# Two layers of graph attention on 4096 nodes: node rows grouped by partition, and the scale of the exponentials computed on another engine

## What is computed

```
h = relu(layernorm(x))                                   # per row of 128
cos = beta * (h @ h.T) / (norm(h) @ norm(h).T + 1e-7)
P = softmax(cos + (1 - adj) * -1e9, axis=1)              # only edges count
x = x + P @ h
h = relu(layernorm(x))
x = x + h @ W_self + (adj @ h / max(rowsum(adj), 1)) @ W_neigh
```

## Time and profile before

| | |
|---|---|
| Time, median of 3 runs | 494.0 us (493.81 to 495.3) |
| Profiled execution | 493.64 us, span 491.8 us |
| TensorE busy | 467.5 us, 95% of the span |
| VectorE, ScalarE, GpSimd busy | 281.5, 285.3, 288.5 us |
| Granted TensorE clock | 0.999 of full speed |
| Moved by DMA | 74.37 MB in 31548 packets |

### The profile page before, as it was taken

The page is one execution under the profiler, slowest core; times in us unless marked ns, Lnnn a source line. Parts: engine busy times, 40 slices in busy tenths (PEclk is TensorE's granted clock), DMA queues, the critical chain, the costliest instruction groups (busy, mean ns, idle before and its releaser), DMA issues.

```text
span 491.8 us, 12379 instructions
## 1 busy us (share of the span) xinstructions
PE 467.5 (95%) x5200; PEld 391.3 (80%) x5200; DVE 281.5 (57%) x675; ACT 285.3 (58%) x425; POOL 288.5 (59%) x250
## 2 busy tenths in 40 slices
PE   1869999999999999999999999998999999999997
PEld 1737888888787887888878877886787888888886
DVE  6977756657566585566855675775766410122222
ACT  2998778775886767966589669777864100000000
POOL 3899988876986768975699569767762000000000
PEclk9999999999999999999999999999999999999999
DMA  8246964456676445855567556655300000000000
GB/s 251 105 130 221 313 253 178 174 213 197 216 291 217 176 139 196 290 199 189 176 227 256 158 194 216 212 195 175 107 5 0 13 13 23 23 23 23 23 23 21
DMA packets 31548, 74.37 MB, mean 151 GB/s; under 512 B 2560, under 2 KB 15104, under 8 KB 31488
## 3 DMA queue, kind: packets, MB, share of 16 engines
q1 hardware_dynamic: 31488, 73.54, 43.8%
HBM read 71.43 MB, written 2.10 MB: 150 GB/s over the span
## 4 chain that ended last, share of the span: by engine, by line
PE 89%; DVE 4%; POOL 3%; issue 1%; DMA 1%; ACT 1%; SPq 0%; DVEq 0%; POOLq 0%
PE ps L1131 23%; PE ps L1008 17%; PE ps L1019 10%; PE ps L1114 7%; PE ps L1111 7%; PE ps L1113 6%; PE ps L1086 5%; PE ps L1089 5%; PE ps L1088 5%; POOL adj_t L419 1%; DVE adj_t L668 1%; DMA x_sb<-in_x_dram 1%; PE ps L1043 1%; POOL adj_t L408 1%; PE ps L1058 1%
## 5 line engine op out<-in xcount | busy, mean ns | idle before, releaser
L434 POOL TENSOR_TENSOR near<-word,adj_t 128x1024 f32<-128x1024 f32 x72 | 145.5, 2021 | 69.8 <-DVE word L813 66.0
L581 ACT ACTIVATE word<-ps,small 128x512 f16<-128x512 f32 x144 | 135.3, 940 | 78.9 <-PE ps L1008 73.3
L813 DVE TENSOR_TENSOR word<-ps,word 128x512 f16<-128x512 f32 x144 | 106.3, 738 | 93.2 <-ACT ps L582 93.1
L1131 PE MATMUL ps<-table,adj_t 128*128 128x257 f16 x1024 | 114.7, 274 | 0.0
L1008 PE MATMUL ps<-unit_t 128*128 128x512 f16 x432 | 107.0, 379 | 4.3 <-DVE word L813 2.3
L1131 PEld LDWEIGHTS ps<-table,adj_t 128*128 128x128 fp8e4 x1024 | 100.0, 98 | 13.5
L582 ACT ACTIVATE ps<-ps,small 128x512 f32<-128x512 f32 x144 | 106.9, 742 | 0.0
L1111 PE MATMUL ps<-table,near 128*128 128x129 f16 x576 | 102.6, 219 | 1.9 <-POOL near L434 1.8
L1114 PE MATMUL ps<-table,near 128*128 128x129 f16 x576 | 102.9, 222 | 0.0
L1113 PE MATMUL ps<-table,near 128*128 128x128 f16 x576 | 102.6, 219 | 0.0
L1086 PE MATMUL ps<-table,far 128*128 128x129 f16 x448 | 79.9, 219 | 0.2
(11 more groups left out here) (87 smaller groups left out, 442.5 us busy)
## 6 DMA issues: line engine op xcount, KB each, us to landing
stage<-in_adj_dram SPq DMA_DIRECT2D x128, 512.0 KB, 4.3
x_sb<-in_x_dram SPq DMA_DIRECT2D x4, 512.0 KB, 6.0
x_again<-in_x_dram SPq DMA_DIRECT2D x7, 256.0 KB, 6.1
out_dram<-x_sb SPq DMA_DIRECT2D x7, 256.0 KB, 4.0
far<-in_x_dram SPq DMA_DIRECT2D x1, 256.0 KB, 3.3
out_dram<-x_sb SPq DMA_DIRECT2D x1, 192.0 KB, 2.1
adj_t<-in_L_gnn_W_neigh_dram SPq DMA_DIRECT2D x1, 64.0 KB, 7.5
adj_t<-in_L_gnn_W_self_dram SPq DMA_DIRECT2D x1, 64.0 KB, 7.6
```

The costliest lines, as they stand in the source:

```text
L434: pool.tensor_tensor(ring(near, k), ring(word, k), adj_t[:, near_adj(k)], ALU.mult).then_inc(s_near, 1)
L581: act.activation(half(word16, k, c, 0, HIGH, TPS), score(k, c), ACT.Exp, bias=exp_bias, scale=exp_scale)
L813: dve.tensor_tensor(half(word16, k, c, 0, LOW, TPS), score(k, c), half(word16, k, c, 0, HIGH, TPS), ALU.subtract).then_inc(s_elo, 1)
L1131: return pe.matmul(ps[:, agg_bank(g, t), 0:TW], adj_t[:, at:at + P], tab(b), start=(b == 0), stop=(b == T - 1))
```

## The change

Nodes are laid out so that partition p holds rows 32p to 32p + 31 of x, not the rows p, p + 128, and so on. The views of x and of the output change by that, and so does the packing of the edge tiles before the launch. Beta's load goes from SP's queue to ScalarE's, and the operations on it go from VectorE to GpSimd, where they are eight in place of seven. ScalarE waits for their end before its first exponential.

```diff
-    x_v = x_in.rearrange("(t p) d -> p t d", p=P)
-    out_v = out.rearrange("(t p) d -> p t d", p=P)
+    x_v = x_in.rearrange("(p t) d -> p t d", p=P)
+    out_v = out.rearrange("(p t) d -> p t d", p=P)
...
         def _(sp):
-            sp.dma_start(beta, beta_in.partition_broadcast(P)).then_inc(s_beta, 16)
             for i in range(XP):
...
+            pool.wait_ge(s_beta, 16)
+            pool.tensor_tensor(b_sq, beta, beta, ALU.mult).then_inc(s_scale, 1)
+            pool.wait_ge(s_scale, 1)
+            pool.tensor_scalar(b_zero, b_sq, 1e-36, 1e-18, ALU.is_le, ALU.mult).then_inc(s_scale, 1)
+            pool.tensor_scalar(b_keep, b_sq, 1e-36, 1.0, ALU.is_gt, ALU.mult).then_inc(s_scale, 1)
+            pool.tensor_scalar(b_pos, beta, 0.0, -1.0, ALU.max, ALU.mult).then_inc(s_scale, 1)
+            pool.wait_ge(s_scale, 4)
+
+            pool.tensor_tensor(beta_s, beta, b_keep, ALU.mult).then_inc(s_scale, 1)
+            pool.tensor_scalar(exp_bias, b_pos, 1.0, E_BITS * LN2, ALU.mult, ALU.add).then_inc(s_scale, 1)
+            pool.wait_ge(s_scale, 6)
+            pool.tensor_tensor(beta_s, beta_s, b_zero, ALU.add).then_inc(s_scale, 1)
+            pool.wait_ge(s_scale, 7)
+            pool.tensor_scalar(exp_scale, beta_s, 1.0 / (HS * HS), None, ALU.mult).then_inc(s_scale, 1)
             inverse_std(0)
...
         def _(act):
+            act.dma_start(beta, beta_in.partition_broadcast(P)).then_inc(s_beta, 16)
             act.preload_act_table(ACT.Exp)
...
+            act.wait_ge(s_scale, 8)
             act.wait_ge(s_flag, 1)
...
-            dve.wait_ge(s_beta, 16)
-            then(dve.tensor_tensor(b_sq, beta, beta, ALU.mult))
-            then(dve.tensor_scalar(b_zero, b_sq, 1e-36, 1e-18, ALU.is_le, ALU.mult))
-            then(dve.tensor_scalar(b_keep, b_sq, 1e-36, None, ALU.is_gt))
-
-            then(dve.scalar_tensor_tensor(beta_s, beta, b_keep, b_zero, ALU.mult, ALU.add))
-            then(dve.tensor_scalar(exp_scale, beta_s, 1.0 / (HS * HS), None, ALU.mult))
-
-            then(dve.tensor_scalar(b_pos, beta, 0.0, None, ALU.max))
-            then(dve.tensor_scalar(exp_bias, b_pos, -1.0, E_BITS * LN2, ALU.mult, ALU.add))
             row_sums(0)
...
-    flipped = adj.T
+    flipped = adj.reshape(128, n // 128, 128, n // 128).transpose(3, 2, 1, 0).reshape(n, n)
```

More of the change, by code:

```diff
@@ L261, in gnn_program @@
         s_beta = sem("beta_loaded")
+        s_scale = sem("exp_scale_step")
         s_w = sem("weights_loaded")
```

## The result

The changed kernel takes 494.79 us (median of 20 runs, 494.42 to 496.4) where the kernel before takes 493.82 (20 runs, 493.75 to 495.31). The ratio is 1.0018, with a 95% interval of 1.001 to 1.0026: a slowdown of 0.9 us, small and clear of noise. A small gain had been forecast.

What follows compares the result with a forecast made beforehand. TensorE was taken as the bound from 45 us, x's landing before it. 493.64 - 0.45 (SP) - 0.15 (contiguous source) = 493.04, from the median 493.4; predicted 493.2 us, range 492.1 to 494.8.

Steps and rivals of the forecast that it cites:

- What bounds the kernel: Whole run: TensorE bounds it from 45 us on; before that everything hangs on x's landing, whose shift reaches the end.
- Beta's load leaves SP: Start, SP's queue: without beta's load the x loads are issued at 0.73, 0.45 us earlier; ScalarE's idle time covers its issue.
- x in consecutive rows: First x loads: a contiguous DRAM source speeds landing by 0.15 us, between bounds of nothing and 0.64.
- GpSimd's eight operations: Start, GpSimd: eight small beta steps take 2.2 us, end at 5.7 and cost nothing, with 1.8 us to spare.
- B = 5.4: Start, GpSimd: beta's landing time B from which its steps, ending at B + 2.2, make GpSimd late and decide the chain.
- VectorE's seven: Start, VectorE: removing its seven beta operations, from 3.55 to 4.90, gains 0.03 us at most.
- x_again, stores, order of edges: Residual reads, output stores and edge packing: each taken as 0; bounds 0.3 gain for reads, 0.6 loss for stores.
- (a): Start: two engines' loads are turned into packets one after the other, x lands at about 5.32; 493.6 or 494.0; chance 0.18.
- (d): First x loads: reads stepping 16 KB between partitions run slower, at half rate 497.4 us; chance 0.04.
- (c): Start: beta lands late beside x and GpSimd holds the chain; 494.3 to 497.8 us; chance 0.08.

Runs made afterwards that it cites:

- e11: The changed kernel with beta loaded as one 4-byte piece to one partition and spread by a TensorE product; 493.35 us at full clock.
- e5: The kernel before with beta's load behind the x loads on SyncE and VectorE's seven operations between norms(2) and norms(3); 494.05 us.
- e10: The changed kernel in the old node order, with beta loaded as one 4-byte piece and spread by a TensorE product; 493.07 us at full clock.
- e3: The changed kernel with beta's load put back in front of x on SP; 494.33 us.
- e1: The kernel before with the node order alone changed (x, output, edge tiles); 494.58 us.
- e9: The changed kernel in the old node order, beta on ScalarE's queue and its operations on GpSimd; 495.09 us at full clock, two executions.
- e2: The kernel before with beta's load alone moved to ScalarE's queue, its operations left on VectorE; 495.37 us at full clock.
- e12: The changed kernel with ScalarE's queue loading beta a second time, into an unused column; 494.43 us at full clock.
- e13: e10 with an extra first transfer on ScalarE's queue, 128 pieces of 4 bytes from beta's one address; median 1.8 us above e10's.
- e14: e10 with an extra first transfer on ScalarE's queue, 128 pieces of 8 bytes from different rows of a weight; median 0.7 us above e10's.
- e15: e10 with an extra first transfer on ScalarE's queue, 128 pieces of 512 bytes from one row of a weight; 2.6 us more time.
- e6: e5 with one 64 KB weight load (512-byte pieces) moved to beta's former place on ScalarE's queue; time 0.3 us above e5's.
- e4: The changed kernel with beta's load behind the x loads on SP and GpSimd's eight operations behind convert(0); 496.1 us.

## Why the prediction was wrong

- **What bounds the kernel.** Right. TensorE's 298.47 us from 45 to 345 us are the same, and a shift of x's landing arrives at the end: in the profiled executions 1.45 us at the landing, 1.30 at the third L405, 1.3 of the span.
- **"Beta's load leaves SP", taken at -0.45.** This step failed. x is issued 0.45 us earlier, but beta's 128 reads of one address, side by side with x and not ahead of it, cost 1.36 us (e11 to the change). With the pieces ahead on one queue x took 4.14 us, with none 4.25 (e5): in the old order they were harmless there. The step looked for the price in ScalarE's idle time and never priced what the moved transfer does to its new neighbour. Taken alone, with one piece for beta, the step and all that stays of the change in the old order is worth -0.73 (e10); in the profiled executions it is 0.57, of which x's landing shows 0.31.
- **"x in consecutive rows", taken at -0.15.** This failed in sign. It costs 0.29 without the pieces (e10 to e11) and 0.6 to 0.8 with them ahead of x (e3, e1). With them beside x it costs nothing more, the change is even 0.4 quicker than e9. The packets stayed 512 bytes, as said; the bounds, 0 and -0.64, left out a loss, which stood only among the rivals.
- The three differences along e10 and e11 are -0.73, +0.29 and +1.36. They lead from before to the change step by step, so that they add up to the measured 0.91 at full clock is no proof; by another way the parts differ, as in e9, where beta's load costs 2.0 us in the old order (e10 to e9, with two executions).
- **GpSimd's eight operations.** Right: 2.3 us for 2.2, 1.24 us of idle time behind them. Had x landed at 4.87 as forecast, beta at 5.5 would have held the chain by the rule given (B = 5.4), if by 0.1 us only; since x was later still, it did not.
- **VectorE's seven.** Right, worth nothing here: VectorE stood idle until 6.79.
- **x_again, stores, order of edges.** Right, nothing: 5.9 us to land for 6.1, 1.6 for 1.5.
- **The rivals.** (a) named the interference of two queues, but with "no gain" as its price, and (d) named the reads of x; each had part of the cause. The result lies at the upper edge of the range and between their prices, where no case had been put. (c) had the late beta (4.8 us) and the wrong consequence.
- **The Trainium skill's two rules ("DMA: Bandwidth & Descriptors", sections "Issuing engines are not separate DMA queues" and "Specifications").** That transfers of several engines interleave is borne out by the 437 and 89 packets side by side from 3 to 5 us; that only issue time is at stake is not, since interleaving with a broadcast read cost the neighbour 1.36 us. That 512-byte pieces are at line rate was beside the point: x's pieces never changed.

Open: why a run of eight rows in a partition delays the start of a transfer; why order and queue do not add (e2 and e9 are slower than the change); and why a second copy of beta's pieces (e12) costs nothing. Open too: what of e13's and e14's medians is x's and what late beta's. That reading one address is what hurts x is shown by its landings in e13 against e14 and in e15 against e6, one execution each, and by e15's time; by what path, is not.

## What to carry to other kernels

Load a scalar that all partitions need as one piece and spread it on an idle engine (0.7 us here, e10); if it must be a broadcast read, keep it out of the time in which a load on the chain is under way on another queue, even where nobody waits for it. When a transfer moves to another queue, price what it will run beside, not only who issues it and who waits for it. Rearranging DRAM rows for longer runs gained nothing here while the SBUF side stayed cut, and the start of the transfer got slower.

## What was unexpected of the hardware

- 128 reads of one DRAM address on one queue halved the rate of a 512 KB load on another: 152 GB/s in place of 322 (e11) over 1.9 us, with the DMA engines at 0.59 of their time. In e13 the transfer starts late instead: 2 GB/s from 2.0 to 2.5 us, where e10 has 103. With 512-byte pieces it lasted longer: 0.28 MB in 3 us against 0.77.
- TensorE's clock in the kernel's start: in some executions of every kernel the mean clock is lower, and where a profile caught one (e4, e11), about half is granted, the 1.2 GHz level, for some 4 us after a stretch in which TensorE idled for much of the time (1.26 us of work in 4 in e4, 2.07 in e11, then 0.57). It costs most such executions 1.1 to 1.7 us, more than the change itself; in e5 and e6, where the clock falls earlier, their medians are 0.1 to 0.2 us up. How often it happens differs, 7 of 7 executions in e4 and 1 of 12 in e14, but what decides it is not shown: before and e11 did the same 2.07 us of work and only e11 fell.
